# A four-layer fused kernel: orders of small pieces on VectorE, ScalarE and GpSimd around the linear attention layer

## What is computed

```python
x = x + _L0_attn_ref(_layernorm(x), ...)   # causal softmax attention, 16 heads, 4 key/value heads
x = x + _L0_ffn_ref(_layernorm(x), ...)    # second layernorm, ternary weights, bias
x = x + _L1_attn_ref(_layernorm(x), ...)   # linear attention: A = sum over tokens of K/|K| * V,  Y = A * rope(Q), W_out
x = x + _L1_ffn_ref(_layernorm(x), ...)    # silu(gate) * up, down; weights are integers, scaled
```

```python
QKV = jnp.einsum('bsd,ed->bse', X, W_in) + b_in
Q, K, V = jnp.split(QKV, 3, axis=-1)
Q = rope(Q, rot_dim)
K = rope(K, rot_dim)
A = jnp.sum(feature_map(K) * V, axis=-2)   # feature_map divides each row by its norm
Y = A[:, None, :] * Q
Y = jnp.einsum('bsd,ed->bse', Y, W_out) + b_out
return Y + X
```

## Time and profile before

| what | value |
|---|---|
| median of 3 runs | 578.76 us (578.47 to 580.87) |
| the profiled execution | 580.42 us, of which span 578.6 us |
| PE busy | 562.7 us (97%) |
| DVE busy | 469.3 us (81%) |
| ACT busy | 370.7 us (64%) |
| POOL busy | 220.5 us (38%) |
| granted TensorE clock | 0.998 |

### The profile page before, as it was taken

One profiled execution on the slowest core, in us unless ns is written; L12 is line 12 of the kernel. 1 busy time (PEld: TensorE's weight loads), 2 busy tenths in 40 slices (PEclk: granted clock), 3 DMA queues, 4 the chain that ended last, 5 costly groups with the idle time before them and its releaser, 6 DMA issues.

```text
span 578.6 us, 12867 instructions
## 1 busy us (share of the span) xinstructions
PE 562.7 (97%) x4131; PEld 530.6 (92%) x4131; DVE 469.3 (81%) x1475; ACT 370.7 (64%) x1037; POOL 220.5 (38%) x324
## 2 busy tenths in 40 slices
PE   8999999999999999999999999999998999999995
PEld 7899999999999999999999999999998888778884
DVE  5888789778877987897789779977887999778875
ACT  5987566657655666575567657557876777454452
POOL 4782224233322522342232233323457678503320
PEclk9999999999999999999999999999999999999999
DMA  8806000000000000000000000000000000001011
GB/s 330 289 1 228 2 2 2 1 1 0 0 0 0 0 0 0 0 0 0 0 0 0 0 0 0 0 0 1 1 1 2 0 2 1 2 0 37 23 33 57
DMA packets 9152, 14.71 MB, mean 25 GB/s; under 512 B 1568, under 2 KB 6688, under 8 KB 9120
## 3 DMA queue, kind: packets, MB, share of 16 engines
q1 hardware_dynamic: 9120, 14.30, 7.0%
HBM read 12.20 MB, written 2.10 MB: 25 GB/s over the span
## 4 chain that ended last, share of the span: by engine, by line
PE 80%; DVE 10%; ACT 5%; issue 3%; POOL 1%; DMA 0%; DVEq 0%; SPq 0%; POOLq 0%
PE bank L651 65%; PE bank L737 5%; PE bank L753 4%; PE bank L756 2%; PE bank L661 2%; ACT prob L1143 1%; PE bank L866 1%; DVE raw L1787 1%; DVE xn_b L1754 1%; DVE prob L1552 1%; DVE qkv L1767 1%; ACT raw L1339 1%; DVE pT L1498 1%; ACT big L1116 0%; DVE oT L1498 0%
## 5 line engine op out<-in xcount | busy, mean ns | idle before, releaser
L526 POOL TENSOR_SCALAR prob<-prob,rowinv 128x256 f32<-128x256 f32 (+1 forms) x127 | 96.3, 770 | 266.1 <-DVE rowinv L1568 266.1
L651 PE MATMUL bank<-xT,big 128*128 128x256 f32 x984 | 129.7, 284 | 0.1
L651 PEld LDWEIGHTS bank<-xT,big 128*128 128x128 f32 x984 | 123.4, 192 | 1.0 <-issue 0.3
L1143 ACT ACTIVATE prob<-prob,negmax 128x128 f32<-128x128 f32 (+1 forms) x256 | 112.8, 445 | 8.3 <-DVE negmax L1552 8.3
L651 PE MATMUL bank<-wp,oT 128*128 128x256 f32 x768 | 102.5, 283 | 0.3 <-DVE oT L1498 0.3
L651 PEld LDWEIGHTS bank<-wp,oT 128*128 128x128 f32 x768 | 96.8, 190 | 1.1 <-DVE oT L1498 0.5
L1105 ACT ACTIVATE qT<-bank 128x512 fp32r<-128x512 f32 x68 | 40.6, 597 | 72.1 <-PE bank L651 72.0
L651 PE MATMUL bank<-pT,v 128*128 128x512 f32 (+1 forms) x384 | 79.8, 343 | 1.2 <-DVE pT L1498 1.2
L651 PEld LDWEIGHTS bank<-pT,v 128*128 128x128 f32 x384 | 63.2, 189 | 10.2 <-issue 1.4
L1498 DVE TENSOR_TENSOR pT<-bank,pT 128x512 fp32r<-128x512 f32 (+1 forms) x128 | 65.2, 551 | 2.9 <-ACT pT L1105 2.9
L1105 ACT ACTIVATE pT<-bank 128x512 fp32r<-128x512 f32 (+1 forms) x128 | 55.2, 484 | 12.1 <-PE bank L753 10.0
(11 more groups left out here) (186 smaller groups left out, 962.2 us busy)
## 6 DMA issues: line engine op xcount, KB each, us to landing
raw<-in_wq SPq DMA_DIRECT2D x4, 512.0 KB, 7.1
raw<-in_wp SPq DMA_DIRECT2D x4, 512.0 KB, 7.5
x<-in_x SPq DMA_DIRECT2D x7, 256.0 KB, 7.2
out<-x SPq DMA_DIRECT2D x7, 256.0 KB, 2.1
raw<-in_w_gu SPq DMA_DIRECT2D x2, 640.0 KB, 5.0
raw<-in_w_in SPq DMA_DIRECT2D x1, 768.0 KB, 4.7
raw<-in_w_down SPq DMA_DIRECT2D x1, 640.0 KB, 6.7
raw<-in_wk SPq DMA_DIRECT2D x1, 512.0 KB, 4.0
```

What stands on the lines that cost most here:

```text
L526: m = pool.tensor_scalar(prob[:, j % 2, 0, a:b], prob[:, j % 2, 0, a:b], rowinv[:, j % 2, r:r + 1], None, ALU.mult)
L651: m = pe.matmul(out, lhs(a), rhs(b), start=first and i == 0, stop=last and i == len(passes) - 1, skip_group_check=True)
L1143: m = act.activation(prob[:, j % 2, i, a:b], prob[:, j % 2, i, a:b], ACT.Exp, scale=-1.0, bias=negmax[:, 2 * i + r:2 * i + r + 1], accum_o ...
```

## The change

Six things move; no computation is added or taken away. On DVE, `linear_moments(6)` goes from step 5 to the end of step 6 of the last image, the first piece of the down weights from linear(3) to linear(2), and in linear(7) `add_bank(5)` from ahead of gated_x_lo(0) to behind linear_sum(6). On ACT, `linear_x_hi(n+1)` stands ahead of `k_squares(n)`, and the gated layer's first silu ahead of linear_y(7). On POOL, `linear_scale(6)` goes from step 4 of the last image to linear(3), and two waits on `s_ln` are new: the third and fourth piece of GU0 wait until linear_apply(1) is done, and the last piece of GU1 until linear_apply(6) is done.

```diff
--- before.py
+++ after.py
@@ -567,8 +567,9 @@
                             in_weights_lo(IN0 if j == 2 else IN1)
                         if j == 4:
                             for part in range(4):
+                                if part == 2:
+                                    pool.wait_ge(s_ln, 2)
                                 gated_weights_lo(GU0, part)
-                            linear_scale(NB - 2)
                         if j == 6:
                             for part in range(3):
                                 gated_weights_lo(GU1, part)
@@ -605,9 +606,12 @@
                     linear_bias(n - 1)
                 if n == 2:
                     ternary_bias(NB - 1)
+                if n == 3:
+                    linear_scale(NB - 2)
                 if n == 4:
                     linear_scale(NB - 1)
                 if n == 5:
+                    pool.wait_ge(s_ln, NB - 1)
                     gated_weights_lo(GU1, 3)
                 if n == NB - 2:
                     gated_inv_std()
@@ -1362,9 +1366,9 @@
                     act.activation(yT[:, e, :], q_sb[n % 2][:, e, :], ACT.Copy, scale=A_sb[:, e:e + 1]).then_inc(s_ly, 1)
 
             def linear(n):
+                linear_x_hi(n + 1, (n + 1) % 2) if n + 1 < NB else gated_x_hi(0)
                 if n > 1:
                     k_squares(n)
-                linear_x_hi(n + 1, (n + 1) % 2) if n + 1 < NB else gated_x_hi(0)
                 weigh(n)
                 linear_y(n - 1)
                 linear_q(n)
@@ -1460,8 +1464,8 @@
             linear_residual(1)
             for n in range(1, NB):
                 linear(n)
+            gated_silu(0, 0)
             linear_y(NB - 1)
-            gated_silu(0, 0)
             hidden_hi(0, 0)
 
 
@@ -1646,13 +1650,13 @@
                         if j == 5:
                             linear_apply(1)
                             o_lo(n, j)
-                            linear_moments(NB - 2)
                         if j == 6:
                             invert_sums(n, J - 1)
                             normalise(n, J - 1)
                             q_products(0)
                             o_lo(n, j)
                             linear_x_lo(1, 1)
+                            linear_moments(NB - 2)
                     if j == J - 1 and last:
                         k_copy(0)
                         k_cosine(0)
@@ -1811,19 +1815,24 @@
                     k_cosine(n)
                     if n == NB - 2:
                         ln_moments(NB, 0)
-                    add_bank(n - 2, bY, s_lo, s_lres, s_la)
-                    linear_x_lo(n + 1, (n + 1) % 2) if n + 1 < NB else gated_x_lo(0)
-                    if n == NB - 1:
+                    if n < NB - 1:
+                        add_bank(n - 2, bY, s_lo, s_lres, s_la)
+                        linear_x_lo(n + 1, (n + 1) % 2)
+                        linear_sum(n - 1)
+                    else:
+                        gated_x_lo(0)
                         gated_apply(1)
-                    linear_sum(n - 1)
+                        linear_sum(n - 1)
+                        add_bank(n - 2, bY, s_lo, s_lres, s_la)
                 else:
                     linear_sum(n - 1)
                     linear_x_lo(n + 1, (n + 1) % 2)
                     k_cosine(n)
                     ternary_moments(NB - 1)
+                if n == 2:
+                    down_weights_lo(0, 3 * D, DOWN0)
                 if n == 3:
                     add_bank(NB - 1, bO, s_fp, s_fb, s_fa)
-                    down_weights_lo(0, 3 * D, DOWN0)
                 if n == 4:
                     linear_moments(NB - 1)
                 if n == 5:
```

## The result

| what | before | after |
|---|---|---|
| median of 9 runs each | 580.36 us (578.47 to 580.87) | 576.96 us (576.09 to 578.38) |
| ratio after / before | | 0.995, 95% interval 0.9939 to 0.9962 |
| the profiled execution | 580.42 us, span 578.6 | 577.33 us, span 575.4 |
| PE busy | 562.7 us | 562.1 us |

The kernel became 0.5% faster. The median stands at the 577.1 us of the forecast, and that is luck: the three runs of before that I had seen had a median of 578.76, and with six more it is 580.36, so my starting point was 1.6 us low and my gain 1.5 to 1.7 us small, and the two cancel. I had subtracted 1.7 us; the medians differ by 3.4 us, the spans of the two profiled executions by 3.2. Most of this text is on where the other 1.5 us came from.

The account below looks back on a forecast made before the run. PE, busy 97% of the span, was taken as the bound, its 4.9 us of waits as ceiling. Entry 0, linear layer -0.5 (+0.3 carried inside) and silu -1.24 made -1.7 us, from 578.76 to 577.1; range 575.0 to 579.0.

Parts of the forecast that it names:

- likeliest case: Whole kernel: a gain of 1.7 us to 577.1 us, by itself 576.3 to 578.0; chance 0.46.
- Part 1: End of attention: PE's 1.21 us wait vanishes but comes back; entry into the linear layer 0, bounds -1.21 and +0.93.
- rival in which the lock bites at the entry: Entry into the linear layer: DVE's second half sits behind a POOL instruction, 0.8 us later, 577.9 us; chance 0.12.
- Part 2: Down weights one image earlier: PE waits some 0.5 us before image 4's transposes, given back later; value 0.1 us.
- Part 3: ACT's x parts ahead of squares: saves DVE 0.4 us per image, chain over weigh not shortened; +0.3 us to linear(7).
- Part 4: POOL's linear_scale(6) in linear(3) and waits before gate pieces: moved at no price, the last gate piece never waits.
- Part 5: Linear(7), second gated apply ahead of the addition: PE's 1.26 us wait vanishes, weigh(7) limits the gain to -0.5 us.
- Part 6: Start of gated layer, silu ahead of linear_y(7): table load runs in ACT's idle time, PE's kT wait vanishes, -1.24 us.

Follow-up runs that it names:

- e4: Changed kernel with moments(6), linear_scale(6) and the third GU0 piece's missing wait at the end of attention as before; 577.39 us, ratio 0.9957.
- e7: Changed kernel with the moments of image 6 later still, behind k_cosine(0); 576.36 us, ratio 0.9939.
- e3: Changed kernel with the first piece of the down weights back in linear(3); 577.14 us, ratio 0.9951.
- e10: Kernel before with only linear_x_hi(n+1) moved ahead of k_squares(n) on ACT; 578.27 us, ratio 0.997.
- e2: Changed kernel with k_squares(n) ahead of linear_x_hi(n+1) on ACT again; 578.39 us, ratio 0.9971.
- e9: e2 with POOL's last gate piece waiting for the apply of image 7; 577.86 us, ratio 0.9961.
- e5: Changed kernel with add_bank(5) ahead of gated_x_lo(0) in linear(7) again; 576.95 us, ratio 0.9954.
- e6: Changed kernel with linear_y(7) ahead of the first silu again; 578.58 us, ratio 0.997.
- e8: e7 with two later POOL waits: ternary bias addition for the apply of image 4, last gate piece for that of image 7; 575.41 us, ratio 0.9919.

## Why the prediction was right and where it was not

The range and the side held: I gave no resolvable change 0.73 and faster by over 0.5% 0.21, and the ratio lies on that border (0.995, with both sides inside its interval). The likeliest case's gain of 1.7 us was half of what came, and that its time of 577.1 us was met is the luck told above.

**Part 1, the end of attention: the number right, one step wrong.** PE's wait at pT gone, DVE held by the exponential, the pair beside POOL 0.66, the last pT piece at 440.08 against a forecast of 440.0: all this is in the rows, and e4 shows the zero. But I priced the moments at nothing because they fit in DVE's idle 0.98 us. That idle time was a wait for ACT's pT, and this came 1.0 us earlier too, since PE did. The moments then cost 0.94 us (e7), which is what this stretch would have won. The rival in which the lock bites at the entry (0.8 us later) didn't come.

**Part 2, the down weights: right in mechanism, 0.2 us off.** I forecast an end of the apply at about 460.9 (measured 458.16 + 2.64 = 460.80) and a wait of PE of 0.5 (0.35). It is given back, and slightly more: -0.11 us instead of +0.1 (e3). I had not seen that PE also waits 0.46 us for linear_y on ACT in that image. That wait comes with the x parts (e10 has it, e2 doesn't), and it cost nothing: k_copy(3) in e10 stands where it stood before, to 0.01 us.

**Part 3, x parts ahead of squares: the step that failed.** I wrote that the chain over weigh "doesn't shorten", and carried +0.3 us into linear(7). Measured by the end of weigh(7), 495.71 less the shift of 0.05, against 496.73 before, it was -1.07 us. k_copy(n) on DVE shows where: less the shift it stands 0.35 and 0.23 us earlier than before in linear(4) and (5), and 1.06 in linear(6). The step of 0.83 is the apply in linear(6); e2 loses 0.82 of it there (k_copy(6) at 484.72 - 0.19 = 484.53 against 483.71), and e10 wins 0.86.

Two things were wrong in my step. First, that the apply waits for weigh. e10, where only the x parts moved, shows each apply. That of image 4 does wait, 0.93 us instead of 0.44, and starts where it did. That of image 5 follows the down piece, which loses its lead behind POOL's addition, as told at e10. That of image 6 starts at 473.74 instead of 474.23 and takes 1.33 us instead of 0.92, beside another POOL addition. So up to k_copy(5) next to nothing is won (0.04 us), but only once because of weigh. For the apply of image 7 nothing takes the lead away: in before it started 0.50 us behind the end of weigh(5), held up by DVE's own queue with the wait of 0.40 us for the x part in it.

Second, a DVE that comes 0.4 us earlier meets POOL in another order, and I left that out. I had counted the collision in linear(3), where DVE's own piece moved, and did not go through the same pair of queues at the second down piece, where nothing had been moved on either. The Trainium skill says in "SBUF — State Buffer", Who interferes with whom: "Issue order, not op shape, decides who blocks." The traces agree: the same two DVE and three POOL instructions end for DVE 0.8 us earlier or later by whether its down piece starts together with POOL's k_rotate or 0.49 us behind it, 0.38 of it in the start of the apply and 0.43 in its length. e9 shows by itself that the gate piece beside the apply is 0.61 us of the 0.8; the remaining 0.2 fits with the earlier start of the apply, which no run separates.

What I had weighed was whether the squares come later. In linear(4) they started at 470.52 instead of 470.57, though k_copy(4) was 0.35 us earlier, and without the shifts 0.23 us later than in e2. So the hold-up of 0.2 us that I forecast is there, but weigh(4) starts in both at the same time (within 0.04 us), and it cost nothing. The wait of 0.9 us for qT near 488 that I expected to stay fell to 0.3 us, and is 0.9 again in e2.

**Part 4: right.** The gate piece starts at 482.15, right behind the bias addition, and did not wait. e4 shows that linear_scale(6) costs nothing in its new place, together with its neighbours.

**Part 5, the gated apply: size right, cause half wrong.** Against weigh I forecast -0.8 us and the next bound, weigh(7), and both came: linear_sum(7) starts 0.05 us behind weigh(7), where 0.79 us had lain between them, so -0.74. But the edit that I had credited is worth nothing (e5). The wait in linear(7) hung on ACT's x part behind the squares; e2, with the addition moved and the x part not, keeps the wait of 1.26 us, and e10, with the x part moved and the addition not, has 0.4. So the -0.74 belongs to part 3's edit too, and makes with linear(6)'s 0.82 the 1.5 us of e2.

**Part 6, silu ahead of linear_y: right, 0.2 us too small.** From linear_sum(7) to the down product the changed kernel gains 3.21 - 1.81 = 1.40 us against the forecast 1.24. The 0.16 us between them is a wait that I had not counted: before, PE's weight load at 506.38 waited that long for the late hidden tile, as it does in e6. Load, silu and hidden tile came in the forecast order (load 497.36, silu 500.46, hidden tile at 501.73 behind the moments), 0.9 to 1.6 us earlier than I wrote, also because all of linear(7) was earlier.

The sum by measured terms: -1.81 at linear_sum(7), where I had 0 + 0.3 - 0.8 = -0.5, and -1.40, where I had -1.24: together -3.21 instead of -1.74. Of the 1.47 us between them 1.31 lie ahead of linear_sum(7): the +0.3 that parts 2 and 3 carried was -1.07, which is 1.37 off, and part 5 gave 0.06 less than forecast. The other 0.16 are part 6. By the experiments nearly all of this is part 3's: part 2 is worth -0.1 (e3), part 1 nothing (e4).

What stays open is why an apply stretches to just these lengths (1.69, 1.88, 2.31, 2.64 us) beside different POOL instructions; I can order them roughly by how many POOL instructions run beside them, but I missed by 0.4 us when I forecast one in e8.

## What to carry to other kernels

When an edit makes an engine arrive earlier, follow it through every later place where its instructions run beside those that stretch them, here DVE beside POOL, and not only where the code was changed. In linear(5) a copy that came 0.4 us earlier changed who was first, and 0.8 us of its 1.5 us lie there; in linear(3) the same 0.4 us were lost again behind a POOL addition (e10). Ask at each such place, too, what the next instruction really waited for before, and whether an idle time that is to hide something moves with the edit. In this kernel's hand-written order the copies that only need the previous matmul belong ahead of the ones that wait for a chain of other engines, and a function's table load ahead of anything that waits. And a stall removed from the list of waits is worth what the next bound leaves: the moments and the addition each took a wait out of PE's list here and gave nothing (e4, e5).

## What the runs showed of the hardware

Two pairs of DVE and POOL instructions that look alike behave unlike: two DVE instructions of 128x128 beside two of POOL took 0.66 us instead of 0.55 (435.85), while two of 128x256 beside two POOL additions of 128x512 took 2.64 (458.16), against 0.73 for an equal pair that met no addition (493.44). So the short pair went through nearly undivided, and the long one did not.

A small instruction can pay as much as a large one: DVE's 128x2 tensor_scalar for the gated layer's variance took 1.01 us beside POOL's bias addition of 1.28, and 0.17 us at 450.41, where no POOL instruction ran beside it:

```profile
488.41 1.28 POOL L460 TENSOR_TENSOR x<-x,biases 128x512 f32<-128x512 f32 x1
...
488.70 1.01 DVE L1863 TENSOR_SCALAR ternary_variance<-ternary_moments 128x2 f32<-128x2 f32 x1
```

And a table load on ACT (1.28 us) starts ahead of the wait of the activation that needs it: in the changed kernel it ran at 497.36, 3.1 us before silu at 500.46, whose data was not there yet.
